# First attention layer: third turning bank from the first step, inverse sums read in another round, large loads behind waits

## The reference

```
# layer 0: grouped-query cross attention; 32 query heads of 16, 8 key/value heads
q = x @ Wq + bq;  k = ctx @ Wk + bk;  v = ctx @ Wv + bv
scores = einsum('bkgld,bksd->bkgls', q, k) / sqrt(16) + mask      # mask: B x 1 x 512 x 1024
out = einsum('bkgls,bksd->bkgld', softmax(scores), v)             # B x 512 x 512
x = layernorm(out @ Wo + bo + x) * gamma + beta
# layer 1: twice (norm, cross attention with 16 heads of 128 and an extra key/value row, residual),
#          then norm, 512 -> 2048 -> gelu -> 512, residual
```

## Time and profile before

| | us |
|---|---|
| time before, median of 3 runs | 2618.31 (2613.81 to 2618.70) |
| the profiled execution's own time | 2616.33 |
| its span | 2614.3 |
| first layer's attention, batch 0 (first maximum to last) | 37.4 to about 278 |
| first layer's attention, batch 1 | 1336.4 to about 1577 |

### The profile page before, as it was taken

How to read it: one execution, slowest core, us unless ns; L and a number is a source line. 1 busy time by engine, 2 the same in 40 slices (tenths; PEclk the granted TensorE clock), 3 DMA queues, 4 the chain that set the end, 5 groups by cost and what they waited for, 6 DMA issues and landing times. The chain is left out here.

```text
span 2614.3 us, 53032 instructions
## 1 busy us (share of the span) xinstructions
PE 2497.5 (96%) x19480; PEld 2063.8 (79%) x19480; DVE 1711.2 (65%) x2600; ACT 1495.2 (57%) x2360; POOL 1310.0 (50%) x746
## 2 busy tenths in 40 slices
PE   6888999999999999999978889999999999999999
PEld 5666688888888888888866666888888888888887
DVE  5999776656657656665269996665666576666541
ACT  5899455555445555545458994555554555554543
POOL 1244246666544666555603433466655446665644
PEclk8999999999999999999989999999999999999999
DMA  7312125354423445442472110334545133544522
GB/s 216 92 58 69 34 71 127 98 124 131 101 73 83 115 103 132 118 113 70 153 173 76 53 67 33 94 104 112 130 111 121 52 99 99 126 128 103 132 71 64
DMA packets 83649, 263.57 MB, mean 101 GB/s; under 512 B 20096, under 2 KB 24336, under 8 KB 77088
## 3 DMA queue, kind: packets, MB, share of 16 engines
q1 hardware_dynamic: 82496, 260.80, 37.6%
q10 hardware_dynamic: 992, 0.52, 0.1%
HBM read 135.39 MB, written 8.40 MB: 55 GB/s over the span
## 5 line engine op out<-in xcount | busy, mean ns | idle before, releaser
L537 POOL TENSOR_TENSOR pT_lo<-pT_lo,pT_hi 128x1024 fp32r<-128x1024 f32 x220 | 529.2, 2406 | 502.2 <-ACT pT_hi L723 496.3
L723 ACT ACTIVATE pT_hi<-pT_lo 128x1024 fp32r<-128x1024 f32 x224 | 237.8, 1062 | 327.4 <-DMA pT_lo<-pb 327.4
L862 ACT ACTIVATE p<-ps_s,nm 128x1024 f32<-128x1024 f32 x256 | 284.7, 1112 | 205.5 <-DVE nm L1755 204.9
L1752 DVE TENSOR_REDUCE nmx<-ps_s 128x1 f32<-128x1024 f32 x256 | 309.7, 1210 | 121.9 <-PE ps_s L1071 121.9
L1071 PE MATMUL ps_s<-kT,qT 128*128 128x512 f32 x1536 | 383.6, 392 | 0.0
L1771 DVE STREAM_TRANSPOSE pb<-p 128x1024 f32<-128x1024 f32 x224 | 278.2, 1242 | 105.8 <-ACT p L862 101.6
L1071 PEld LDWEIGHTS ps_s<-kT,qT 128*128 128x128 f32 x1536 | 281.3, 188 | 55.4 <-ACT p L862 1.0
L1676 DVE CUSTOM_DVE_ANT_0 sm<-ps_s,mask 128x1024 f32<-128x1024 f32 x256 | 305.4, 1213 | 19.5 <-PE ps_s L1193 15.5
L815 ACT ACTIVATE p<-sm,nm 128x1024 f32<-128x1024 f32 x256 | 293.2, 1145 | 19.1 <-DVE nm L1676 15.3
L1071 PE MATMUL ps_t<-ctxT,wa 128*128 128x512 f32 x1080 | 255.9, 390 | 0.0
L1071 PE MATMUL ps_m<-hT,wa 128*128 128x512 f32 x1008 | 243.5, 393 | 0.7 <-ACT g L1033 0.7
(11 more groups left out here) (181 smaller groups left out, 4664.2 us busy)
## 6 DMA issues: line engine op xcount, KB each, us to landing
pT_lo<-pb SPq DMA_DIRECT2D x896, 128.0 KB, 2.3
stg_qk<-in_wqk SPq DMA_DIRECT2D x40, 1024.0 KB, 7.4
stg_vo<-in_wo SPq DMA_DIRECT2D x48, 512.0 KB, 3.6
wob<-in_wo SPq DMA_DIRECT2D x32, 512.0 KB, 3.6
stg_vo<-in_wv SPq DMA_DIRECT2D x32, 512.0 KB, 3.6
q_stack<-scr_q SPq DMA_DIRECT2D x48, 128.0 KB, 4.2
st_ctx<-in_ctxT SPq DMA_DIRECT2D x8, 512.0 KB, 6.2
scr_q<-parts SPq DMA_DIRECT2D x8, 512.0 KB, 6.2
```

Of the source, the lines that this page charges most:

```text
L537: return nc.gpsimd.tensor_tensor(out, x, f32(hi), ALU.subtract)
L723: return nc.scalar.activation(out, in_, ACT.Copy)
L862: nc.scalar.activation(p[t % 2][:], ps_s[t % 2][:], ACT.Exp, bias=nm[:, i:i + 1], scale=SCALE1, accum_out=sums[:, i:i + 1]).then_inc(exp_d ...
L1752: nc.vector.tensor_reduce(nmx[:, i:i + 1], ps_s[t % 2][:], AX.X, ALU.max, negate=True)\
```

## The change

The last two query parts go into the second halves of the score tiles; their waits for a free bank go. The bank pattern holds from the first half on; PE waits for all six parts once, ahead of the first scores. The low part 5 follows the low part 4 directly. ScalarE's copy of the turned inverse and VectorE's multiplication stand in the round t % 8 == 3. SP waits for value group 4 ahead of x_res, 6 ahead of acc, 7 ahead of the second wob, and w0o goes behind the fourth wob. POOL's add_row moves to unit 3 and its value rows to units 4 to 15.

```
-ROWS_OF_UNIT = (0, 0, 0, 1, 1, 1, 2, 1, 1, 2, 1, 1, 2, 1, 1, 1)
+ROWS_OF_UNIT = (0, 0, 0, 0, 1, 1, 2, 1, 2, 1, 2, 1, 2, 1, 1, 1)
...
-        bank0 = [ps_m[0][:], ps_m[1][:], ps_s[0][:, 0:512], ps_s[1][:, 0:512], ps_m[0][:], ps_m[1][:]]
+        bank0 = [ps_m[0][:], ps_m[1][:], ps_s[0][:, 0:512], ps_s[1][:, 0:512],
+                 ps_s[0][:, 512:1024], ps_s[1][:, 512:1024]]
         turn_banks = [*ps_t, ps_m[1]]
-        bank_of_half = [h % 2 if h < UNIT else (0, 1, 2, 0, 2, 1, 0, 2)[h % 8] for h in range(2 * STEPS0)]
+        bank_of_half = [(0, 1, 2, 0, 2, 1, 0, 2)[h % 8] for h in range(2 * STEPS0)]
...  SyncE
+                def after_group(n):
+                    sp.wait_ge(pv0_done, b * (STEPS0 // GROUPS) + n)
+                    apart()
+
+                after_group(4)
                 sp.dma_start(x_res[:], d["x"][b, :, :, :]).then_inc(xres_in, 16)
                 load_row(b * ROWS, 0)
-                sp.dma_start(w0o[:], d["w0o"]).then_inc(w0o_in, 16)
...
+                after_group(6)
                 sp.dma_start(acc[:], d["rows1"]).then_inc(acc_in, 16)
                 for f in range(V_B):
+                    if f == 1:
+                        after_group(7)
+                    if f == 4:
+                        sp.dma_start(w0o[:], d["w0o"]).then_inc(w0o_in, 16)
                     load_wob(b, f)
...  GpSimd
-                    if u == 2:
+                    if u == 3:
                         pool.wait_ge(xres_in, 16 * (b + 1))
...  ScalarE
                     copied0(t - 1, 0)
                     if t + 2 < STEPS0:
                         exp0(t + 1)
-                    copied0(t, 0)
-                    if t + 2 < STEPS0:
-                        exp0(t + 2)
                     if t % UNIT == GROUPS - 1 and t > UNIT:
                         u = t // UNIT - 1
                         act.wait_ge(rb0_filled, b * UNITS0 + u + 1)
                         copy(rb0[u % 2][:], inverse0(u)).then_inc(rb0_done, 1)
+                    copied0(t, 0)
+                    if t + 2 < STEPS0:
+                        exp0(t + 2)
...  TensorE
-                    if i >= 2:
-                        free(nb + i)
...
-                pe.wait_ge(bank_free, nb + 6)
+                pe.wait_ge(bank_free, nb + U_PROJ0 + 2)
...
                             pe.wait_ge(t0_copied[before[1]], t0 + before[0] + 1)
-                        elif bank_of_half[2 * t + q] == 2:
-                            pe.wait_ge(bank_free, nb + U_PROJ0 + 2)
...  VectorE
-                for i in range(3, 5):
+                for i in range(3, 6):
                     low_part(i)
...
                         maxima0(t + 1)
-                    if t % UNIT == GROUPS + 1 and t > UNIT:
-                        normalised(t // UNIT - 1)
                     if t + 2 < STEPS0:
                         maxima0(t + 2)
                     copied0(t - 1, 1)
                     copied0(t, 1)
-                    if t == 1:
-                        low_part(5)
+                    if t % UNIT == GROUPS - 1 and t > UNIT:
+                        normalised(t // UNIT - 1)
                     if t % UNIT == UNIT - 1:
                         inverse(t // UNIT)
```

## The result

| | before | changed |
|---|---|---|
| median, us | 2616.26 (4 runs, 2613.81 to 2618.70) | 2591.64 (4 runs, 2587.94 to 2592.66) |
| profiled execution, us | 2616.33 | 2592.66 |
| its span, us | 2614.3 | 2590.6 |

The ratio is 0.9903, 95% interval 0.9886 to 0.9921: 24.6 us faster by the medians (0.94%), between 21 and 30 by the interval. The forecast was 2597 within 2591 to 2607, from a gain of 20.2 us: the sign is right and so is the stage in which the time is won, the size is a fifth short, and two of the three terms are wrong in opposite directions.

The account below looks back on a forecast made before the run. VectorE was taken to bound the first layer, PE the second, so only VectorE's idle 28.6 us could be won. Gains of 8.0 + 5.6 + 6.6 = 20.2 us gave a forecast of 2597 us, within 2591 to 2607.

Parts of the forecast that it names:

- Edit 1: First steps of each batch: third turning bank from step one, query columns in the scores' banks; gain 8.0 us.
- Edit 2: Each unit of 8 steps: inverse sums read in another round, removing VectorE's gaps; gain 5.6 us of 6.87.
- Edit 3: Large loads set apart behind value groups, so the hole at step 15 goes; gain 6.6 us of 7.07.
- The reading of the hole: Step 15 of each batch: PE out of instructions because its fetch stood behind large loads; 7.07 us of VectorE's time.
- rival A: The hole is not the loads' or comes again at another burst; gain 13.6, about 2604 us; chance 0.13.
- The low end: Whole kernel: all idle time gone but the unavoidable wait for the second scores, about 25.5 us, so 2591.
- Rival B: Beginning stays bound by low clock and DMA, gaining 3 instead of 8.0 us; about 2602 us; chance 0.08.
- step 8: Sign in the first steps: DVE's maximum of step 8 comes 15.7 us after the first one (19.5 before).
- Rival C: First layer slower: POOL makes r0 late, PE waits; 39 us late in all, about 2636 us; chance 0.04.
- D: No change within 0.2%: new PE holes at the three bursts take 21 us; about 2617 us; chance 0.05.
- the clock before 53: Sign at the beginning: PE's clock rises before 53 us.
- under 1.5 us of idle VectorE: Sign in the first layer: DVE idle under 1.5 us in steps 24 to 127.

Follow-up runs that it names:

- banks_sums: Changed kernel but with the large loads placed as before: ratio 0.9909 to the kernel before, 23.8 us faster.
- experiment 2: Changed kernel with 64 semaphore increments in TensorE's stream ahead of its wait for the first stacks: 2592.83 us, ratio 0.9901 to the kernel before.
- experiment 3: Changed kernel with w0o (1 MB) issued right behind x_res and its row again: 2591.06 us, one execution.
- only_loads: Kernel before with only the large loads set apart, banks and sums as before: ratio 0.9977, 6.0 us faster.
- experiment 5: Changed kernel with acc after group 5, x_res and w0o in quarters behind wob loads, add_row in unit 13: 2587.57 us, ratio 0.9889 to the kernel before.

## Why the prediction was right or wrong

**What bounds the kernel: right.** The first layer is VectorE's: with its idle time gone a unit takes 14.20 us while VectorE's operations are the same. The second layer kept the gain whole: it went by within 1.4 us of before in two batches.

**Edit 1, the banks: right.** 8.0 us forecast, 8.1 by the trace (15.41 for "15.7 us after the first one"), 7.6 in the same steps alone, where the whole kernel gained 9.4 (5.2 to 13.6). The clock rose in the stretch 48 to 52 where the forecast had 52:

```profile
48.00:52.00 4.00, 4.00 (x76) 3.20 (x72) 3.32 (x7) 3.30 (x7) 0.00 (x0) 0.65 1.08 139
```

The wait for all six parts cost nothing: the first scores still waited for q_stack's DMA, 3.37 us (3.30 before).

**Edit 2, the sums: the mechanism right, the term mis-sized.** 5.6 us forecast out of 6.87 of idle time, with 6.87 as the upper end; it brought 13.6 (9.7 to 17.5) alone, and 28 steady units with 0.42 us make 11.8 of it. The step that failed is "only the gaps count: 3.03 + 3.84". Span minus busy undercounts the gaps: a copy counts as busy 0.69 us but the next instruction starts after 0.60 when it can, and a maximum counts 1.22 and is followed after 1.14. VectorE's timeline of the kernel before, around the wait of 0.18 in the earlier trace rows:

```profile
104.20 0.68 DVE L1684 COPY pt<-ps_t 128x512 f32<-128x512 f32 x1
...
105.67 1.22 DVE L1676 CUSTOM_DVE_ANT_0 sm<-ps_s,mask 128x1024 f32<-128x1024 f32 x1
106.81 0.08 DVE L1676 DVE_READ_ACCUMULATOR2_ANT nm<- 128x1 f32 x1
106.95 1.22 DVE L1676 CUSTOM_DVE_ANT_0 sm<-ps_s,mask 128x1024 f32<-128x1024 f32 x1
```

The copy at 104.20 would let the next start at 104.80; it starts at 105.06 and has lost 0.26, not 0.18. The maximum at 105.67 would let the next start at 106.81; it starts at 106.95, 0.14 late, of which 0.06 count as idle. Together 0.40 a unit, where the idle time has 0.24. The right reading was open: 8 x (1.14 + 0.60) + 0.20 + 0.11 for the two small operations = 14.2 us from start to start a unit, against a period of 14.64.

**Edit 3, the loads: the step "I leave 0.5 us for all bursts: gain 6.6" failed.** The reading of the hole was right, and alone the edit brought 6.0. But in the changed kernel the hole stands again at the next burst, 2.71 and 2.03 us, with 0.82 at step 19 ahead of it, which is not x_res's: 5.6 us instead of 0.5. That leaves 1.5 us for the term, which agrees with banks_sums (1.6, within its scatter). This is the mechanism of rival A ("a fetch may stand at just that place"), given 0.13, and 5.1 of the 6.6 us at which it was priced; I had weighed the bytes and not the place. Where the stream moves by 64 instructions the burst costs nothing (experiment 2), and without any move it is a matter of how long ago the last fetch was served (table of experiment 3). That only_loads alone brought 6.0, close to 6.6, is therefore luck: in its batch 0 the fetch started at 80.8, and x_res was issued at 80.80.

The Trainium skill's rule (page "Runtime: NRT & Kernel Launch", section "Instruction fetch mechanics") that fetching is "mostly hidden" holds in the 190 us of experiment 5 that go by with 0.01 us of idle VectorE. Beside full queues it does not always hold: PE stood 0.9 to 4.5 us a time in these traces.

**The sum** came near the result because an undersized term (5.6 for about 12) and an oversized one (6.6 for 1.5) lie against each other: 20.2 forecast, 23.7 by the spans. That is luck. The low end, 2591, was worked out as "all idle time gone", and the changed kernel reached it with holes still in it, for the same undercount. Rival B (beginning stays bound by the low clock) is refuted by step 8. Rival C did not happen: VectorE was idle 0.31 us in 176, which leaves no room for PE waiting for r0. Nor did D, whose 21 us would have taken back all three gains (20.2), not only the banks' and the loads' (14.6) as its text says.

Of the signs that the prediction named, these came out: step 8, the clock before 53, under 1.5 us of idle VectorE behind the holes (0.5 and 0.4 us in 180), and a first layer of 231.4 and 230.5 us from first maximum to last, where it was 241.1. "No PE idle over 1 us by issue" failed with 1.89 and 1.21 us, and the sign against it, a hole beside the x_res burst, came.

**Left open:** by how much the low clock itself holds up the first steps, since the kernel made for it moved the fetches too; and how often a hole stands in the executions that have no trace.

## What to carry to other kernels

Where an engine is the bound, take the achievable period from start-to-start distances of its operations when nothing waits, not from the span minus its busy time. Before moving a large load, place it against the instruction fetches of the stream that others wait for: a burst that holds one up costs, the same burst 64 instructions off did not, and any edit that lengthens that stream can bring such a hole back. Spreading the loads in small pieces over a quiet stretch gave the best kernel here, but only for the bursts that were spread. When several engines hand a value on, move the whole chain: each half alone gave nothing or lost.

## What the runs showed of the hardware

- TensorE stood by issue for 0.9 to 4.5 us where large loads or many small ones filled the DMA queues and an instruction fetch was served late. In the changed kernel the fetch started at 83.2, 5.3 us behind x_res's issue, and TensorE went on at 85.65; the 31 value products behind the stand took 1.93 us, at a granted clock of 0.50.
- With a fetch started 0 to 0.9 us ahead of the issue of a 1 MB load there was no such stand (4 cases); with the last one 3.5 to 4.0 us ahead there was one of 0.97 to 3.26 us (4 cases).
- 64 semaphore increments in TensorE's stream went with a stand of 5.87 us ahead of the first scores instead of 3.37, and it ended by issue and no longer by q_stack's DMA: the increments took longer than the wait they were put into.
- 40 turnings of the identity kept the granted clock at 1.00 only until 40 us; it was 0.50 from 44 to 48 in the sparse work behind them, 0.51 from 48 to 52 (0.65 in the changed kernel) and 1.00 from 52 on, as in the changed kernel.
